# Moving the second part's mask work from VectorE to GpSimd and ScalarE

## The chip, the cores and the metric

The kernel runs on one core of one Trainium2 chip. The metric is the device time of one execution in microseconds (us), median of three runs. A core has five engines that run side by side and meet only at semaphores: TensorE (PE in the profile), VectorE (DVE), ScalarE (ACT), GpSimd (POOL) and SyncE (SP), which issues most of the DMAs.

## The reference

128 graphs of 64 nodes with 256 features go through two graph networks. The first is one attention layer with 8 heads. The second, which this case is about, has 3 layers, each with one attention head and a feed-forward part:

```
mask = adjacency.astype(float32) + eye(n) > 0          # self loops added
for l in range(3):
    scores = si[:, :, None] + sj[:, None, :] + attn_b[l]
    scores = where(scores >= 0, scores, 0.2 * scores)
    scores = where(mask, scores, -inf)
    attn   = softmax(scores, axis=-1)
    h      = layernorm(x + attn @ x, g1[l], beta1[l])
    x      = layernorm(h + gelu(h @ W1[l] + b1[l]) @ W2[l] + b2[l], g2[l], beta2[l])
```

`adj` holds int32 zeros and ones. The mask depends on the graph alone, so one mask serves all three layers.

## The kernel before

Two graphs share the 128 partitions. Four such pairs (512 nodes) are a group; there are 16 groups. The first part goes over 64 pairs in a loop and leaves its result in memory. The second part takes the groups four at a time: a lap is 4 groups times 3 layers, 12 units, and there are 4 laps, so 48 units U = 0 to 47. The unit within a lap is `s`; `layer_group(s)` gives its layer (`s // 4`) and group (`s % 4`).

Each unit has 8 chunks, c = 0 to 7. A chunk is a product with W1 into a PSUM bank (`hidden`, L773, 6 matmuls with 512 columns), a gelu in place (`gelu`, ACT L874), a rounded copy (`high`, ACT L879, tile hid_hi), its remainder (`low`, DVE L1057, tile hid_lo), and, two chunks later, a product with W2 (`output`, L797, 12 matmuls with 256 columns). After the eighth `hidden` TensorE runs `output` for chunks 5, 6 and 7 one behind the other; the last of them needs `low` of chunk 7.

Between the chunks each engine runs, in an order written out by hand, the attention of coming units. On DVE (`some` in `second_vector`): sums and statistics, `scores` of unit U + 2 (L1139 to L1147), and for U + 3 `make_mask` (only if that unit is of layer 0), `dots_of` (8 dot products a unit, L1100: one between chunks 6 and 7, in two instructions, and three pairs behind chunk 7) and `diagonal`. On POOL (`some` in `second_gpsimd`): `make_base`, `scale_y`, `finish` (last layer only), `scale_n`, `post`. On ACT, exp of U + 2 at the end of the unit.

`make_mask(i, s)` waits for the group's load (`s_in`), adds `node_of` (a float tile with 1 on the diagonal) to the int32 adjacency into `mask_sum` (L1109), and turns zeros into -1e30 and the rest into 0 (L1112), in `mask`, which stays for three layers. It runs between `low` of chunks 4 and 5 in the units 9 to 12, 21 to 24 and 33 to 36, once in the middle and once late in unit 0, and twice in the tail of the first part: 16 times. In other units it adds 2 to the semaphore `s_sc` by itself (`dve.sem_inc`).

The first part's last ten steps (`tail(tau)`, tau from NT = 64 on) are mixed with the start of the second part. TensorE's `bias` products (L812) stand there too.

## Time and profile before

| | |
|---|---|
| median of 3 runs | 1536.05 us (1535.99 to 1536.13) |
| profiled execution, its own time | 1535.7 us |
| its span, first to last instruction | 1533.5 us |
| PE busy | 1490.6 us, 97% |
| PEld busy | 1272.8 us, 83% |
| DVE busy | 1390.3 us, 91% |
| ACT busy | 1102.2 us, 72% |
| POOL busy | 898.8 us, 59% |
| granted TensorE clock, mean | 0.987 |

How to read it: busy is time with an instruction of that engine under way. The share is a mean over the whole span; what bounds a stretch is seen where an engine stops and for whom it waits. Engines run their own lists in order, so a wait holds everything that stands behind it in that list.

### The profile page before, as it was taken

Reading aid. Unit: us, or ns where it says so; the run is one execution under the profiler, and the core shown is the slowest. Engines: PE = TensorE matmul, PEld = TensorE weight load, DVE = VectorE, ACT = ScalarE, POOL = GpSimd, SP = SyncE. Lnnn points to the kernel's source line nnn. Section 1 sums busy time; section 2 is a strip of 40 time slices with the busy share of each in tenths; the row PEclk is TensorE's granted clock in tenths of the full one; section 3 lists DMA queues with packets and bytes.
Section 4 is the critical chain, followed back from the end, with each engine's and each line's share of the span. In section 5 each row is a group of like instructions: output and inputs, shape, how many; then the busy total and the mean of one; then the engine's idle time right before and its main releaser. Section 6 shows DMA issues by size and latency. Waiting matters only on the chain. (4 is left out here: it accounts for less than half of the span.)

```text
span 1533.5 us, 35213 instructions
## 1 busy us (share of the span) xinstructions
PE 1490.6 (97%) x11360; PEld 1272.8 (83%) x11360; DVE 1390.3 (91%) x4315; ACT 1102.2 (72%) x1948; POOL 898.8 (59%) x1006
## 2 busy tenths in 40 slices
PE   5899999899999999999999999999999999999997
PEld 3677777778888888888989888988888888888887
DVE  7999999879999999999898999898999998989864
ACT  5788888267777767677777676777777677777774
POOL 5799998336463647463636465645455655455565
PEclk9999999599999999999999999999999999999999
DMA  6643334500000102110001121100011211000001
GB/s 199 167 136 124 134 124 132 169 21 15 8 15 10 47 25 87 35 42 8 15 24 33 38 74 42 36 8 15 25 32 40 71 49 29 8 15 8 15 29 55
DMA packets 70890, 82.79 MB, mean 54 GB/s; under 512 B 29280, under 2 KB 54112, under 8 KB 70752
## 3 DMA queue, kind: packets, MB, share of 16 engines
q1 hardware_dynamic: 69120, 74.76, 16.9%
q0 software_dynamic: 816, 3.15, 0.7%
q10 hardware_dynamic: 816, 3.15, 0.5%
q8 instruction: 74, 1.21, 0.3%
q14 instruction: 64, 0.52, 0.1%
HBM read 38.95 MB, written 25.17 MB: 42 GB/s over the span
## 5 line engine op out<-in xcount | busy, mean ns | idle before, releaser
L874 ACT ACTIVATE bank<-bank,b_col 128x512 f32<-128x512 f32 x384 | 252.0, 656 | 282.9 <-PE bank L773 281.7
L797 PE MATMUL bank<-w_hi,hid_hi 128*128 128x256 f32 x1528 | 433.9, 284 | 6.7 <-DVE hid_lo L1057 6.7
L797 PE MATMUL bank<-w_lo,hid_hi 128*128 128x256 f32 x1528 | 431.8, 283 | 0.0
L797 PE MATMUL bank<-w_hi,hid_lo 128*128 128x256 f32 x1528 | 431.8, 283 | 0.0
L1057 DVE TENSOR_TENSOR hid_lo<-bank,hid_hi 128x512 fp32r<-128x512 f32 x384 | 262.2, 684 | 66.6 <-ACT hid_hi L879 65.3
L773 PE MATMUL bank<-nT_hi,w_hi 128*128 128x512 f32 x768 | 317.3, 413 | 1.2 <-DVE nT_lo L1186 1.2
L797 PEld LDWEIGHTS bank<-w_hi,hid_hi 128*128 128x128 f32 x1528 | 291.2, 191 | 22.9 <-DVE hid_lo L1057 9.7
L773 PE MATMUL bank<-nT_lo,w_hi 128*128 128x512 f32 x768 | 303.4, 395 | 0.0
L773 PE MATMUL bank<-nT_hi,w_lo 128*128 128x512 f32 x768 | 301.9, 393 | 0.0
L797 PEld LDWEIGHTS bank<-w_lo,hid_hi 128*128 128x128 f32 x1528 | 291.5, 191 | 11.8
L797 PEld LDWEIGHTS bank<-w_hi,hid_lo 128*128 128x128 f32 x1528 | 291.4, 191 | 0.0
L1007 POOL TENSOR_TENSOR rs_f<-ve_f,minus_half 128x4 f32<-128x4 f32 x47 | 47.8, 1017 | 412.6 <-DVE ve_f L1086 412.6
L1100 DVE CUSTOM_DVE_ANT_0 raw_weights<-xin,att_row 128x256 f32<-128x256 f32 x384 | 240.4, 626 | 10.0
L879 ACT CAST hid_hi<-bank 128x512 fp32r<-128x512 f32 x384 | 225.9, 588 | 10.7
L773 PEld LDWEIGHTS bank<-nT_hi,w_hi 128*128 128x128 f32 x768 | 145.9, 190 | 37.3 <-issue 13.4
L773 PEld LDWEIGHTS bank<-nT_hi,w_lo 128*128 128x128 f32 x768 | 145.0, 189 | 33.5
L773 PEld LDWEIGHTS bank<-nT_lo,w_hi 128*128 128x128 f32 x768 | 146.4, 191 | 16.4
L994 POOL TENSOR_TENSOR raw_weights<-raw_weights,c_row 128x512 f32<-128x512 f32 x96 | 133.4, 1409 | 0.0
L884 ACT ACTIVATE y_tok<-y_tok,nm_f,rs_f 128x256 f32<-128x256 f32 x188 | 102.9, 596 | 35.2 <-POOL nm_f L1009 35.2
L1000 POOL TENSOR_TENSOR rs_a<-ve_a,minus_half 128x4 f32<-128x4 f32 x48 | 48.7, 1014 | 133.4 <-DVE ve_a L1180 133.4
L990 POOL TENSOR_TENSOR raw_weights<-raw_weights,g_row 128x512 f32<-128x512 f32 x96 | 123.4, 1306 | 5.8 <-PE bank L763 4.2
L901 ACT ACTIVATE raw_weights<-raw_weights,nm_a,rs_a 128x256 f32<-128x256 f32 x192 | 99.8, 593 | 5.8 <-POOL nm_a L1002 5.7
(144 smaller groups left out, 3124.5 us busy)
## 6 DMA issues: line engine op xcount, KB each, us to landing
raw_weights<-xin SPq DMA_DIRECT2D x96, 128.0 KB, 2.3
xin<-in_x_dram SPq DMA_DIRECT2D x16, 512.0 KB, 4.0
first_block_out<-x_res SPq DMA_DIRECT2D x16, 512.0 KB, 2.7
second_block_in<-x_act SPq DMA_DIRECT2D x16, 512.0 KB, 3.7
xin<-second_block_in SPq DMA_DIRECT2D x16, 512.0 KB, 3.9
x_fin<-first_block_out SPq DMA_DIRECT2D x16, 512.0 KB, 4.1
out_dram<-x_fin SPq DMA_DIRECT2D x15, 512.0 KB, 2.9
xh_other<-xh SPq DMA_DIRECT2D x128, 33.0 KB, 1.9
```

Of the source, the lines that this page charges most:

```text
L773: mm = pe.matmul(HID[(CF * s + c) % 3][:], w[:, l, k, c * P:(c + 1) * P], a[:, s % 2, k, :], start=(k == 0 and p == 0), stop=(k == KD - 1 ...
L797: mm = pe.matmul(FF[t // 2][:, (t % 2) * D:(t % 2 + 1) * D], a[:, r, t * P:(t + 1) * P], w[:, l, c, :], start=(c == 0 and t % 2 == 0 and p ...
L874: act.activation(h[:], h[:], ACT.Gelu, bias=b1_col[:, l, c:c + 1]).then_inc(s_gelu, 1)
L879: act.copy(hid_hi[:, (CF * s + c) % HRING, :], HID[(CF * s + c) % 3][:]).then_inc(s_hi, 1)
L884: act.activation(y_tok[:, par, t, :], y_tok[:, par, t, :], ACT.Identity, bias=nm_f[:, t:t + 1], scale=rs_f[:, t:t + 1]).then_inc(s_yn, 1)
L901: act.activation(n_tok[:, s % 2, t, :], n_tok[:, s % 2, t, :], ACT.Identity, bias=nm_a[:, t:t + 1], scale=rs_a[:, t:t + 1]).then_inc(s_n, 1)
L990: pool.tensor_tensor(base[:, h], base[:, h], g1_row[:, l].unsqueeze(1).broadcast_to([P, TG // 2, D]), ALU.mult).then_inc(s_base, 1)
L994: pool.tensor_tensor(base[:, h], base[:, h], c1_row[:, l].unsqueeze(1).broadcast_to([P, TG // 2, D]), ALU.add).then_inc(s_base, 1)
L1000: pool.tensor_tensor(rs_a[:], ve_a[:], minus_half[:], ALU.pow).then_inc(s_rsa, 1)
L1007: pool.tensor_tensor(rs_f[:], ve_f[:], minus_half[:], ALU.pow).then_inc(s_rsf, 1)
L1057: dve.tensor_tensor(hid_lo[:, r, :], HID[(CF * s + c) % 3][:], hid_hi[:, r, :].bitcast(F32), ALU.subtract).then_inc(s_split, 1)
L1100: dve.tensor_tensor_reduce(dots, x_cur[:, g, t, :], att_row[:, l, j, :], 1.0, 0.0, ALU.mult, ALU.add, dst[:, t:t + 1]).then_inc(s_dots, 1)
```

## The change

The mask is made by two other engines. At the start DVE makes an int32 copy of the diagonal (`node_int`) and a column `far` with 1e30. POOL adds `node_int` to the loaded adjacency in place (`add_loops`), at the end of its work in the units where DVE made the mask before. ACT makes `mask` as relu(-1e30 * edges + 1e30) between `high` of chunk 1 and `gelu` of chunk 2 of the following unit (`make_mask`, for unit U + 2); it is 1e30 where there is no edge and 0 elsewhere, so `scores` subtracts it. DVE's `make_mask` is gone with the 2-step count; `scores` waits for `s_mask` in layer 0. In the diff the first `make_mask` and the first `tail` are ScalarE's, `add_loops` and the second `tail` GpSimd's, and the removed `make_mask` was VectorE's.

```diff
+        node_int = sb("node_int", [P, N], I32)
+        far = sb("far", [P, 1])
-        mask_sum = in_raw(2048, TG, N)
...
                 dve.tensor_copy(ident_r[:], ident[:]).then_inc(q_identr, 1)
+                dve.memset(far[:], -NEG).then_inc(q_loops, 1)
+                dve.tensor_copy(node_int[:], node_of[:]).then_inc(q_loops, 1)
...
+                def make_mask(i, s):
+                    l, g = layer_group(s)
+                    V = i * SLOTS + s
+                    act.wait_ge(s_edges, V // SLOTS * QG + g + 1)
+                    at_least(act, s_sc, 7 * (V - QG + 1))
+                    act.activation(mask[:, g].rearrange("p t j -> p (t j)"), adj_raw[:, g].rearrange("p t j -> p (t j)"),
+                                   ACT.Relu, bias=far[:], scale=NEG).then_inc(s_mask, 1)
...
                 def tail(tau):
+                    if tau == NT + 4:
+                        act.wait_ge(q_loops, 2)
+                        make_mask(0, 0)
...
                         keep_attn(0, 0)
+                        make_mask(0, 1)
...
                             high(U, s, c)
+                            if nxt2 and c == 1 and layer_group(s + 2)[0] == 0:
+                                make_mask(i, s + 2)
...
+                def add_loops(i, s):
+                    l, g = layer_group(s)
+                    V = i * SLOTS + s
+                    pool.wait_ge(s_in[g], 32 * (V // SLOTS + 1))
+                    pool.tensor_tensor(adj_raw[:, g], adj_raw[:, g], node_int[:].unsqueeze(1).broadcast_to([P, TG, N]),
+                                       ALU.add).then_inc(s_edges, 1)
...
                             post(i, s - 1)
+                        if nxt3 and layer_group(s + 3)[0] == 0:
+                            add_loops(i, s + 3)
+
+                def tail(tau):
+                    if tau == NT + 2:
+                        pool.wait_ge(q_loops, 2)
+                        add_loops(0, 0)
+                    if tau == NT + 5:
+                        add_loops(0, 1)
+                    if tau == NT + 8:
+                        add_loops(0, 2)
...
-                score = Steps(dve, s_sc, 9)
+                score = Steps(dve, s_sc, 7)
...
-                def make_mask(i, s):
-                    l, g = layer_group(s)
-                    V = i * SLOTS + s
-                    score.unit(V)
-                    if l == 0:
-                        dve.wait_ge(s_in[g], 32 * (i + s // SLOTS + 1))
-                        score.done(dve.tensor_tensor(mask_sum, adj_raw[:, g], node_of[:].unsqueeze(1).broadcast_to([P, TG, N]),
-                                                     ALU.add))
-                        score.wait()
-                        score.done(dve.tensor_scalar(mask[:, g], mask_sum, 0.0, NEG, ALU.is_le, ALU.mult))
-                        score.wait()
-                    else:
-                        score.k += 2
-                        dve.sem_inc(s_sc, 2)
...
-                    score.resume(V, 3)
+                    score.resume(V, 1)
                     score.wait()
+                    if l == 0:
+                        dve.wait_ge(s_mask, (V // SLOTS * QG + g + 1))
...
-                                                            mask[:, g, t, :], ALU.add, ALU.add))
+                                                            mask[:, g, t, :], ALU.add, ALU.subtract))
```

DVE's list in unit 10, before. A dot product (L1100) stands as "ISA"; L1057 is `low`, L1139 to L1147 `scores`, L1109 and L1112 the mask, L1186 the remainder of the turned rows.

```order
L1139 SCALAR_TENSOR_TENSOR raw_weights<-bank,src_b,raw_weights 128x64 x4
L1142 SCALAR_TENSOR_TENSOR raw_weights<-raw_weights 128x256
L1144 TENSOR_REDUCE top<-raw_weights 128x4
L1147 TENSOR_TENSOR raw_weights<-raw_weights,top 128x256
L1057 TENSOR_TENSOR hid_lo<-bank,hid_hi 128x512
L1109 TENSOR_TENSOR raw_weights<-adjin,node_of 128x256
L1112 TENSOR_SCALAR raw_weights<-raw_weights 128x256
L1057 TENSOR_TENSOR hid_lo<-bank,hid_hi 128x512
L1186 SCALAR_TENSOR_TENSOR nT_lo<-bank_7,g_col,nT_hi 128x512 x2
L1057 TENSOR_TENSOR hid_lo<-bank,hid_hi 128x512
L1100 ISA raw_weights,s_src<-xin,att_row 128x256
```

The same place in the changed kernel, where `low` is L1093, `scores` L1163 to L1171 and the dot products L1136:

```order
L1163 SCALAR_TENSOR_TENSOR raw_weights<-bank,src_b,raw_weights 128x64 x4
L1166 SCALAR_TENSOR_TENSOR raw_weights<-raw_weights 128x256
L1168 TENSOR_REDUCE top<-raw_weights 128x4
L1171 TENSOR_TENSOR raw_weights<-raw_weights,top 128x256
L1093 TENSOR_TENSOR hid_lo<-bank,hid_hi 128x512 x2
L1210 SCALAR_TENSOR_TENSOR nT_lo<-bank_7,g_col,nT_hi 128x512 x2
L1093 TENSOR_TENSOR hid_lo<-bank,hid_hi 128x512
L1136 ISA raw_weights,s_src<-xin,att_row 128x256
```

`low` of chunks 4 and 5 are now neighbours; nothing else on DVE changes its place.

POOL's list from `post` of unit 9 to `scale_y` of unit 10, before (L967 and L971 `post`, L990 and L994 `make_base`):

```order
L1002 TENSOR_TENSOR nm_a<-ng_a,rs_a 128x4
L967 TENSOR_TENSOR y_tok<-y_tok,g_row 128x512 x2
L971 TENSOR_TENSOR y_tok<-y_tok,beta_row 128x512 x2
L990 TENSOR_TENSOR raw_weights<-raw_weights,g_row 128x512 x2
L994 TENSOR_TENSOR raw_weights<-raw_weights,c_row 128x512 x2
L1007 TENSOR_TENSOR rs_f<-ve_f,minus_half 128x4
```

And in the changed kernel:

```order
L1027 TENSOR_TENSOR nm_a<-ng_a,rs_a 128x4
L985 TENSOR_TENSOR y_tok<-y_tok,g_row 128x512 x2
L989 TENSOR_TENSOR y_tok<-y_tok,beta_row 128x512 x2
L1019 TENSOR_TENSOR adjin<-adjin,node_int 128x256
L1008 TENSOR_TENSOR raw_weights<-raw_weights,g_row 128x512 x2
L1012 TENSOR_TENSOR raw_weights<-raw_weights,c_row 128x512 x2
L1032 TENSOR_TENSOR rs_f<-ve_f,minus_half 128x4
```

The integer add stands between `post` and the next unit's `make_base`.

ACT's list at the start of unit 10 in the changed kernel (L878 gelu, L883 hid_hi, L900 `keep_attn`, L888 `norm_y`); before, the same rows stand there without L907:

```order
L878 ACTIVATE bank<-bank,b_col 128x512
L900 COPY raw_weights<-bank 128x256
L883 CAST hid_hi<-bank 128x512
L878 ACTIVATE bank<-bank,b_col 128x512
L883 CAST hid_hi<-bank 128x512
L907 ACTIVATE raw_weights<-adjin,far 128x256
L878 ACTIVATE bank<-bank,b_col 128x512
L883 CAST hid_hi<-bank 128x512
L888 ACTIVATE y_tok<-y_tok,nm_f,rs_f 128x256 x2
```

No table load stands at the relu; both lists hold 96 table loads in all.

## Rows read from the trace of the kernel before

**Rows 1.** Busy time by stretch: from:to, length, then PE, PEld, DVE, ACT, POOL.

```profile
588.00:619.00 31.00, 30.16 (x203) 26.10 (x202) 30.24 (x92) 21.27 (x35) 15.70 (x14) 1.00 0.15 43
650.00:681.00 31.00, 31.00 (x211) 27.53 (x210) 28.87 (x88) 23.69 (x41) 18.46 (x18) 1.00 0.15 44
```

**Rows 2.** Timeline of PE, `output` where it waited: start, length, engine, line, ..., [idle before].

```profile
332.04 0.39 PE L797 MATMUL bank<-w_hi,hid_hi 128*128 128x256 f32 x1 [1.31 <-DVE hid_lo L1057]
...
562.73 0.39 PE L797 MATMUL bank<-w_hi,hid_hi 128*128 128x256 f32 x1 [0.48 <-DVE hid_lo L1057]
...
588.53 0.39 PE L797 MATMUL bank<-w_hi,hid_hi 128*128 128x256 f32 x1 [0.42 <-DVE hid_lo L1057]
...
1249.20 0.39 PE L797 MATMUL bank<-w_hi,hid_hi 128*128 128x256 f32 x1 [0.42 <-DVE hid_lo L1057]
```

**Rows 3.** Timeline of PE, `turn_n`, once a unit: units 0, 1, 9, 13.

```profile
325.50 1.03 PE L763 MATMUL bank<-ident,raw_weights 128*128 128x128 f32 x8
...
352.66 1.04 PE L763 MATMUL bank<-ident,raw_weights 128*128 128x128 f32 x8
...
554.15 1.03 PE L763 MATMUL bank<-ident,raw_weights 128*128 128x128 f32 x8
...
657.39 1.03 PE L763 MATMUL bank<-ident,raw_weights 128*128 128x128 f32 x8
```

**Rows 4.** Timeline of DVE in unit 10, from the mask on.

```profile
580.29 0.91 DVE L1109 TENSOR_TENSOR raw_weights<-adjin,node_of 128x256 f32<-128x256 int32 x1
581.23 1.27 DVE L1112 TENSOR_SCALAR raw_weights<-raw_weights 128x256 f32<-128x256 f32 x1
582.53 0.69 DVE L1057 TENSOR_TENSOR hid_lo<-bank,hid_hi 128x512 fp32r<-128x512 f32 x1
...
585.06 1.38 DVE L1100 CUSTOM_DVE_ANT_0 raw_weights<-xin,att_row 128x256 f32<-128x256 f32 x1
...
586.48 1.39 DVE L1100 CUSTOM_DVE_ANT_0 raw_weights<-xin,att_row 128x256 f32<-128x256 f32 x1
...
587.80 0.68 DVE L1057 TENSOR_TENSOR hid_lo<-bank,hid_hi 128x512 fp32r<-128x512 f32 x1
588.40 0.41 DVE L1100 CUSTOM_DVE_ANT_0 raw_weights<-xin,att_row 128x256 f32<-128x256 f32 x1
```

**Rows 5.** Timeline of DVE in unit 13, `low` of chunk 7.

```profile
663.97 0.69 DVE L1057 TENSOR_TENSOR hid_lo<-bank,hid_hi 128x512 fp32r<-128x512 f32 x1 [0.19 <-ACT hid_hi L879]
```

**Rows 6.** Groups by line, DVE: count, busy us, mean ns, idle before.

```profile
L1112 DVE TENSOR_SCALAR raw_weights<-raw_weights 128x256 f32<-128x256 f32 x16 | 17.8, 1111 | 0.5
L1109 DVE TENSOR_TENSOR raw_weights<-adjin,node_of 128x256 f32<-128x256 int32 x16 | 13.6, 849 | 0.0
```

**Rows 7.** Groups by line, POOL.

```profile
L469 POOL TENSOR_TENSOR dst_diag<-node_of,a_dst 128x256 f32<-128x256 f32 x128 | 77.2, 623 | 0.0
```

**Rows 8.** Groups by line, ACT: norm with two per-partition columns, exp with none.

```profile
L901 ACT ACTIVATE raw_weights<-raw_weights,nm_a,rs_a 128x256 f32<-128x256 f32 x192 | 99.8, 593 | 5.8 <-POOL nm_a L1002 5.7
L890 ACT ACTIVATE raw_weights<-raw_weights 128x256 f32<-128x256 f32 x48 | 20.1, 418 | 2.0 <-DVE raw_weights L1147 1.4
```

**Rows 9.** Timeline of POOL at the same place: `make_base` behind `post`.

```profile
582.31 2.60 POOL L990 TENSOR_TENSOR raw_weights<-raw_weights,g_row 128x512 f32<-128x512 f32 x2
584.87 2.71 POOL L994 TENSOR_TENSOR raw_weights<-raw_weights,c_row 128x512 f32<-128x512 f32 x2
```

**Rows 10.** Timeline of ACT, gelu of chunk 2 in a unit that follows.

```profile
595.88 0.66 ACT L874 ACTIVATE bank<-bank,b_col 128x512 f32<-128x512 f32 x1 [1.33 <-PE bank L773]
```

**Rows 11.** Timeline of DVE: first mask, in the tail, and the second of unit 0.

```profile
267.04 0.42 DVE L1109 TENSOR_TENSOR raw_weights<-adjin,node_of 128x256 f32<-128x256 int32 x1
...
328.45 1.52 DVE L1109 TENSOR_TENSOR raw_weights<-adjin,node_of 128x256 f32<-128x256 int32 x1
```

**Rows 12.** Timeline of PE in the tail, first matmul of a step.

```profile
269.06 0.47 PE L345 MATMUL bank<-no_edge,ident_r 128*128 128x512 f32 x1 [0.15 <-DVE leaky L527]
```

**Rows 13.** Timeline of DVE at the second part's start, first residual.

```profile
292.56 1.66 DVE L1165 SCALAR_TENSOR_TENSOR raw_weights<-bank,row_inv,xin 128x256 f32<-128x256 f32 x4 [1.61 <-PE bank L754]
```

More of the change, by code:

```diff
@@ L192, in graph_net @@
             q_st = sem("first_stored")
-            q_zero = sem("first_filled")
+            q_zero, q_loops = sem("first_filled"), sem("self_loops_made")
             q_mv, q_rs, q_nmr, q_h = sem("q_mean_var"), sem("q_rstd"), sem("q_shift"), sem("q_h")
@@ L616, in graph_net @@
             s_nT, s_nhi, s_nlo, s_base = sem("nT"), sem("nT_hi_ready"), sem("nT_lo_ready"), sem("base_ready")
+            s_edges, s_mask = sem("edges_with_loops"), sem("mask_made")
             s_b, s_g2, s_c1 = sem("bias_rows_loaded"), sem("g2_rows_loaded"), sem("c1_row_made")
@@ L1046, in after @@
                         pool.tensor_tensor(nm_f[:, half], ng_f[:, half], rs_f[:, half], ALU.mult).then_inc(e_nm, 1)
-                first_gpsimd(pool, lambda tau: None)
+                first_gpsimd(pool, tail)
                 slots(pool, before, some, after)
             def second_vector(dve):
-                score = Steps(dve, s_sc, 9)
+                score = Steps(dve, s_sc, 7)
                 def low(U, s, c):
@@ L1101, in dots_of, with diagonal @@
                                                      ALU.mult, ALU.add, dst[:, t:t + 1]).then_inc(s_dots, 1)
-                def make_mask(i, s):
+                def diagonal(i, s):
                     l, g = layer_group(s)
@@ L1106, in make_mask @@
                     score.unit(V)
-                    if l == 0:
-                        dve.wait_ge(s_in[g], 32 * (i + s // SLOTS + 1))
-                        score.done(dve.tensor_tensor(mask_sum, adj_raw[:, g], node_of[:].unsqueeze(1).broadcast_to([P, TG, N]),
-                                                     ALU.add))
-                        score.wait()
-                        score.done(dve.tensor_scalar(mask[:, g], mask_sum, 0.0, NEG, ALU.is_le, ALU.mult))
-                        score.wait()
-                    else:
-                        score.k += 2
-                        dve.sem_inc(s_sc, 2)
-                def diagonal(i, s):
-                    l, g = layer_group(s)
-                    V = i * SLOTS + s
                     dve.wait_ge(s_dots, 2 * TG * (V + 1))
@@ L1191, in tail @@
                         dve.tensor_copy(same_graph_r[:], same_graph[:]).then_inc(s_samer, 1)
-                    if tau == NT + 3:
+                    if tau == NT + 4:
                         dve.wait_ge(s_w2lo, NT - HEAD)
-                        make_mask(0, 0)
-                    if tau == NT + 4:
                         dve.wait_ge(s_rows, 16 * 3)
@@ L1203, in tail @@
                     if tau == NT + 7:
-                        make_mask(0, 1)
                         dots_of(0, 1, range(0, 2))
@@ L1242, in some @@
                         low(U, s, 1)
-                        if U == 0:
-                            make_mask(0, 2)
                         if nxt:
@@ L1260, in some @@
                             scores(0, 2)
-                        if nxt3:
-                            make_mask(i, s + 3)
                         low(U, s, 5)
```

## The prediction

> **What bounds the kernel now.** I read the busy time by stretch first. Through the second part TensorE is busy in every microsecond of most stretches, as in 650 to 681 us, but not where units 9 to 12 run: in 588 to 619 it is busy 30.16 of 31 us while DVE is busy 30.24 [rows 1]. Elsewhere DVE has some 2 us of air in 31; there it has less than 1. So the kernel is bound by TensorE, and in a few places by DVE.
>
> The timeline of PE then shows what the idle time waits for. In `output` it stops once in each of units 9 to 12, 21 to 24 and 33 to 36, 12 times for 0.42 us (the first 0.48), each time for hid_lo, the work of DVE; and once in unit 0, for 1.31 us [rows 2]. These are just the units in which DVE makes a mask. The first matmul behind a gap also starts the pipeline anew, so the gap is less than the whole loss. The whole loss is read from the period of the units: from unit 1 to unit 9 it is (554.15 - 352.66) / 8 = 25.19 us, from unit 9 to 13 103.24 us for four, or 25.81, and from unit 0 to 1 27.16 us [rows 3].
>
> **How the mask makes the gap.** In unit 10 the two mask instructions take DVE from 580.29 to 582.53, 2.24 us, with `low` of chunk 5 behind them. The list then runs without a rest to `low` of chunk 7 at 587.80 to 588.48 [rows 4], and TensorE, which was ready 0.42 us before 588.53, starts right after it [rows 2]. The control is unit 13: it has no mask, but the rest of a boundary unit (the last layer's extra add on POOL, the load of a new group). There `low` of chunk 7 waits for ACT, not DVE [rows 5], and TensorE has no gap [rows 1]. So the gap is the mask's, not the boundary's.
>
> **The change part by part.** DVE loses 16 times 849 ns and 16 times 1111 ns, 31.4 us of work [rows 6]. What that is worth depends on the place.
>
> Units 9 to 12 and their two repeats: 2.24 us less DVE work ahead of a `low` that was 0.42 us late. DVE stops being last, TensorE's own pace holds, and the period falls from 25.81 to 25.19: 103.24 - 4 x 25.19 = 2.5 us a lap, three laps, 7.5 us. No more than that is had, since TensorE is the next limit at once; the remaining 1.8 us a unit become idle time of DVE. Within ordinary units the period may differ by some 0.1 us with how POOL and DVE meet, so I put 0.8 us on either side of the 7.5.
>
> Unit 0: the mask late in it starts at 328.45, its add takes 1.52 us [rows 11], and the gap behind is 1.31 [rows 2]; the period is 27.16 - 25.19 = 1.97 above the ordinary [rows 3]. `low` of chunks 6 and 7 come closer to the end of ACT's work there, so I take 1.9. The other mask of unit 0 stands ahead of a wait for TensorE and is worth nothing.
>
> The tail: the first mask stands at 267.04 [rows 11], amid the last steps of the first part. TensorE's wait for DVE behind it is 0.15 us [rows 12]; the loop through TensorE and ACT is as tight. Later TensorE works through its bias products, and DVE waits 1.61 us for it at 292.56 [rows 13], so nothing that DVE gains before gets through. I take 0.15; the bounds are 0 and the whole mask, about 1.2 (267.04 to the next instruction).
>
> What is added. POOL gets 16 integer adds of 128x256. The trace has no integer add on POOL; its float product with the same shape and a broadcast operand takes 623 ns [rows 7], and one instruction of `make_base`, with 128x512, 1.3 us [rows 9]. I take 0.65 us and keep 0.3 and 1.3 as ends. It stands right behind `post`, and `make_base` starts at 582.31 without a rest and ends at 587.58 [rows 9]. What needs that is `take_y` of the next unit on DVE, which stands behind `low` of chunk 7 (587.80 to 588.48) and six more dots of 0.41 us [rows 4], so not before 590.9: over 3 us of room cover the shift of 0.65. If the cover were gone, each us would be TensorE's.
>
> The add has a price on DVE as well. A dot product takes 0.41 us when POOL rests and 1.38 when it works: the two between chunks 6 and 7 do the latter, the one behind chunk 7 the former, since POOL ends at 587.58 [rows 4, 9]. With POOL busy 0.65 us longer, one more dot pair meets it and grows by up to 1 us. That is less than the 2.24 us that DVE gives back, and it falls behind `low` of chunk 7, where TensorE has the whole of the next unit's first chunk ahead of it. The two dots before chunk 7 already wait about a whole POOL instruction each (1.38 and 1.39 against 2.71 / 2 = 1.36 [rows 9]), so a shift can hardly make them longer. Sum for this item: 0, bound 0.3 us a unit or 3.6 us.
>
> The Trainium skill (SBUF — State Buffer, Who interferes with whom) has the rule for it: the second port of DVE is shared with GpSimd as an exclusive lock, and the later one waits for the other's whole instruction. By this rule an add costs DVE at most its own length, and only if it is in flight when an instruction with two SBUF inputs comes up; the sum would stay as it is. The trace agrees as far as it goes: the dots grow by about one POOL instruction less their own start.
>
> ACT gets 16 relus of 128x256 with one per-partition column. Exp without a column takes 418 ns, the norm with two 593 [rows 8]; I take 0.5. It stands ahead of the gelu of chunk 2, where ACT waits 1.33 us for TensorE [rows 10]. So it is hidden with 0.8 us to spare; without the cover it would be 12 x 0.5 = 6 us. In unit 0 the gelu of chunk 2 has no such rest, but its `low` comes some microseconds later behind a wait of DVE for TensorE. A table load would break this, at two loads a mask, but the compiled list has none at the relu. POOL's wait for the load stands a unit or more behind the place where the load is issued, as DVE's did. The waits of ACT for POOL's add, and of DVE for the mask, each have a quarter of a unit or more.
>
> The same skill (ScalarE: Activation LUTs, Rules for kernel authors) says to put relu on VectorE, not on ScalarE, because it is faster there. By it the change would be a loss per operation. Here it is the idle engine that counts: ACT is busy 21 us of 31 where DVE is busy 30 [rows 1], and the 849 + 1111 ns on DVE [rows 6] are more than the relu's estimate anyway.
>
> At the start DVE gets a memset and a small copy, below 0.4 us together, while it waits for the first load: 0.
>
> **The sum.** 7.5 + 1.9 + 0.15 = 9.5 us. The profiled execution took 1535.7 us with a span of 1533.5 us; it becomes 1526.2 with 1524.0. The median of the runs lies 0.35 above it: 1526.5 us.
>
> **Rivals.** (a) The lock eats part of it. POOL's instructions land 0.65 us later in units 9 to 12, some dot ahead of chunk 7 waits for one more of them, and `low` of chunk 7 stays 0.3 us late. For it: a dot is three times as long under POOL [rows 4]. Against: the shift moves POOL's ends, not their number, and the dots there are at 1.4 already. Price 12 x 0.3 = 3.6: 1530.1 us.
>
> (b) More comes back than the sum has: the whole 1.2 us of the first mask [rows 11] pass through the tail instead of 0.15, and the 0.8 us of the periods fall to the good side. 1.05 + 0.8 = 1.85 us more: 1524.7 us. For it: DVE does get ahead there, and the steps of the tail hand work back and forth. Against: the 1.61 us wait for TensorE [rows 13].
>
> (c) The change doesn't do what it says: the period of units 9 to 12 belongs to the boundary (new loads, last layer's add on POOL). Then only unit 0 gains: 1534.1 us. Against it stands unit 13 [rows 5].
>
> (d) Slower: POOL's integer add is a slow path. In unit 10 it would start at 582.31 [rows 9]. The first dot behind `low` of chunk 6 waits for its end, the second for the next POOL instruction (1.3 us), and `low` of chunk 7, 0.68 us long, must start by 588.53 - 0.42 - 0.68 = 587.43 for TensorE to have no gap [rows 2, 4]. With 1.3 us for the second dot's wait and 0.5 for its own work, 582.3 + L + 1.8 = 587.4: L = 3.3 us is free. Each us above is lost 12 times. Against the 9.5 us gained (0.8 a unit) it decides from L = 4.1 us. At 5 us: 12 x 1.7 = 20 us lost, 1547 us. Nothing in the trace is near: 623 ns for this shape [rows 7].
>
> **How the numbers follow.** Forecast 0.75, its own range 1525.3 to 1528.0 (0.8 for the periods, 0.4 for unit 0 and the tail, and part of the lock). (a) 0.12, (b) 0.07, (c) 0.03, (d) 0.03. The range of 8 in 10 takes in (a) and the near half of (b): 1524.7 to 1530.5. A difference under 0.2%, 3.1 us, cannot be told from none with a measurement of this kernel. The forecast, (a) and (b) are faster by more than that: 0.93 with a little off for mixtures. Within: (c) and the off part, 0.04. Slower: (d), 0.03.
>
> **What would show it.** Right: no gap of PE for hid_lo in units 9 to 12, 21 to 24, 33 to 36 and at most 0.1 us in unit 0; four periods of 100.7 us where 103.24 stood; `low` of chunk 7 waiting for ACT in these units; POOL's add at 0.6 to 0.8 us; the relu at 0.5 us and the rest before the gelu of chunk 2 shorter by that; DVE busy 31 us less, but for dots grown behind chunk 7. Wrong: gaps left in these units (then (a), with dots ahead of chunk 7 above 1.4 us), an add above 1.3 us, a first residual that moved by more than 1 us from 292.56 to either side (then the tail's 0.15 is wrong).

## The result, and the profile after

The changed kernel takes 1525.41 us (median of 4 runs, 1523.56 to 1525.83) against 1536.02 us for the kernel before (4 runs, 1535.93 to 1536.13), a ratio of 0.9929 with the 95% interval 0.9911 to 0.9946. The forecast was 1526.5 us. The profiled execution took 1523.56 us, the shortest of the four; its span is 1521.7 us, 11.8 us less than before.

From the page of the changed kernel: the busy line, then three groups (busy us and mean ns of one behind the first bar, idle time ahead of them behind the second).

```profile
PE 1485.7 (98%) x11360; PEld 1270.5 (83%) x11360; DVE 1369.0 (90%) x4285; ACT 1108.9 (73%) x1964; POOL 911.4 (60%) x1022
...
L801 PE MATMUL bank<-w_hi,hid_hi 128*128 128x256 f32 x1528 | 432.1, 283 | 0.1
...
L1093 DVE TENSOR_TENSOR hid_lo<-bank,hid_hi 128x512 fp32r<-128x512 f32 x384 | 261.1, 683 | 77.5 <-ACT hid_hi L883 76.6
...
L1136 DVE CUSTOM_DVE_ANT_0 raw_weights<-xin,att_row 128x256 f32<-128x256 f32 x384 | 246.9, 643 | 10.0
```

TensorE no longer waits in `output` (0.1 us in all, 6.7 before), and `low` (L1093) waits 76.6 us for ACT, where it was 65.3 before. The stretch of busy time that answers to [rows 1], in the changed kernel:

```profile
588.00:619.00 31.00, 31.00 (x218) 27.00 (x218) 29.18 (x89) 22.05 (x38) 18.18 (x18) 1.00 0.15 44
```

TensorE is busy in all 31 us, and DVE, busy 29.18 us, has some air. The periods come from the same instruction as in [rows 3], `turn_n`, here for units 0, 1, 9 and 13 of the changed kernel (start, us, engine, line):

```profile
323.55 1.04 PE L767 MATMUL bank<-ident,raw_weights 128*128 128x128 f32 x8
...
349.04 1.04 PE L767 MATMUL bank<-ident,raw_weights 128*128 128x128 f32 x8
...
550.45 1.03 PE L767 MATMUL bank<-ident,raw_weights 128*128 128x128 f32 x8
...
650.95 1.04 PE L767 MATMUL bank<-ident,raw_weights 128*128 128x128 f32 x8
```

Units 9 to 12 take 100.50 us (103.24 before), unit 0 25.49 (27.16), units 1 to 8 201.41 (201.49). Over the whole span, read in this way:

| stretch | before | after | gain |
|---|---|---|---|
| four units with masks, three laps | 103.24, 103.19, 103.19 | 100.50, 100.60, 100.51 | 8.0 |
| period of unit 0 | 27.16 | 25.49 | 1.67 |
| first `turn_n` to that of unit 0 | 25.53 | 23.99 | 1.54 |
| start of the first `turn_n` | 299.97 | 299.56 | 0.41 |
| all other units | 830.42 | 830.25 | 0.2 |

The third row was not in the prediction. In it the granted clock differs. The last three numbers of each line are the granted clock, the DMA share and GB/s, first for the kernel before, then for the changed one:

```profile
307.00:310.00 3.00, 1.66 (x5) 0.94 (x4) 0.00 (x0) 2.94 (x4) 2.05 (x2) 0.82 0.45 126
310.00:313.00 3.00, 2.07 (x7) 1.74 (x8) 1.10 (x3) 2.96 (x5) 2.90 (x3) 0.75 0.02 7
313.00:316.00 3.00, 3.00 (x22) 2.61 (x25) 1.32 (x3) 1.88 (x4) 0.00 (x0) 0.68 0.00 0
...
308.10:308.60 0.50, 0.50 (x3) 0.13 (x1) 0.00 (x0) 0.47 (x2) 0.50 (x1) 1.00 0.38 143
```

```profile
307.00:310.00 3.00, 1.64 (x4) 0.72 (x3) 0.00 (x0) 2.94 (x4) 3.00 (x3) 0.72 0.53 143
310.00:313.00 3.00, 2.48 (x15) 2.23 (x16) 1.10 (x3) 2.96 (x6) 1.66 (x2) 1.00 0.00 0
313.00:316.00 3.00, 3.00 (x28) 2.12 (x27) 1.83 (x4) 1.77 (x4) 0.00 (x0) 1.00 0.01 3
...
308.10:308.60 0.50, 0.50 (x2) 0.00 (x0) 0.00 (x0) 0.47 (x2) 0.50 (x1) 0.50 0.58 135
```

The engine comes out of a stretch at half its full clock (1.2 of 2.4 GHz, 0.50). Before, it rises and falls back once more before it stays up; after, it rises and stays. The last line of each group shows another difference: TensorE works until 308.6 us in both and then waits about 2 us for ACT, but before, the clock is up while it still works, and after, it comes up only when the work has ended.

The added work, all 16 of each (shortest, median and longest in ns), and where they run in unit 9 and the start of unit 10 of the changed kernel:

```profile
L1019 POOL TENSOR_TENSOR adjin<-adjin,node_int x16: 716/733/922, 265.9 to 1232.2; 128x256 int32<-128x256 int32 x16
L907 ACT ACTIVATE raw_weights<-adjin,far x16: 494/512/531, 272.4 to 1243.4; 128x256 f32<-128x256 int32 x16
```

```profile
552.55 0.74 POOL L1019 TENSOR_TENSOR adjin<-adjin,node_int 128x256 int32<-128x256 int32 x1
553.25 2.54 POOL L1008 TENSOR_TENSOR raw_weights<-raw_weights,g_row 128x512 f32<-128x512 f32 x2
```

```profile
554.22 0.69 DVE L1093 TENSOR_TENSOR hid_lo<-bank,hid_hi 128x512 fp32r<-128x512 f32 x1 [1.00 <-ACT hid_hi L883]
554.83 1.25 DVE L1136 CUSTOM_DVE_ANT_0 raw_weights<-xin,att_row 128x256 f32<-128x256 f32 x1
...
556.11 1.40 DVE L1136 CUSTOM_DVE_ANT_0 raw_weights<-xin,att_row 128x256 f32<-128x256 f32 x1
...
557.44 0.68 DVE L1093 TENSOR_TENSOR hid_lo<-bank,hid_hi 128x512 fp32r<-128x512 f32 x1
558.04 0.91 DVE L1136 CUSTOM_DVE_ANT_0 raw_weights<-xin,att_row 128x256 f32<-128x256 f32 x1
...
582.16 0.69 DVE L1093 TENSOR_TENSOR hid_lo<-bank,hid_hi 128x512 fp32r<-128x512 f32 x1 [0.35 <-ACT hid_hi L883]
```

```profile
564.22 0.51 ACT L907 ACTIVATE raw_weights<-adjin,far 128x256 f32<-128x256 int32 x1
565.65 0.66 ACT L878 ACTIVATE bank<-bank,b_col 128x512 f32<-128x512 f32 x1 [0.92 <-PE bank L777]
```

In unit 9 `low` of chunk 6 (554.22) waits 1.00 us for ACT, where before it had no rest. `low` of chunk 7 (557.44) still starts right behind a dot, 6.99 us after the unit's `turn_n`; before it was 7.85. So of the 2.24 us taken off DVE only 0.86 reach it, and most of the rest is that wait ahead of it. In units 10 to 12 it waits for ACT, 0.35 us in unit 10 (582.16), 0.25 and 0.16 in the next two; over the three laps it does so in 7 of the 12 units. The dot behind it is 0.91 us in unit 9 instead of 0.41, as POOL works longer.

### The profile page after: what moved, and what is told of

Its sections match the earlier page's. It is cut to its first block, busy times and chain, and to the rows that moved or that the text cites. A ratio compares the mean times of both kernels' runs of the same rounds, so it can differ in the third digit from the quotient of the medians.

```text
span 1521.7 us, 35183 instructions
## 1 busy us (share of the span) xinstructions
PE 1485.7 (98%) x11360; PEld 1270.5 (83%) x11360; DVE 1369.0 (90%) x4285; ACT 1108.9 (73%) x1964; POOL 911.4 (60%) x1022
## 4 chain that ended last, share of the span: by engine, by line
PE 94%; DVE 2%; DMA 1%; issue 1%; ACT 1%; SPq 0%; POOL 0%; ACTq 0%; DVEq 0%; POOLq 0%
PE bank L801 36%; PE bank L777 35%; PE bank L758 3%; PE bank L361 3%; PE bank L351 3%; PE bank L767 3%; PE bank L319 2%; PE bank L336 2%; PE bank L349 2%; DMA adjin<-in_adj_dram 1%; PE bank L329 1%; PE bank L346 1%; PE bank L816 1%; PE bank L746 1%; PE bank L738 0%
## 5 line engine op out<-in xcount | busy, mean ns | idle before, releaser
L878 ACT ACTIVATE bank<-bank,b_col 128x512 f32<-128x512 f32 x384 | 251.9, 656 | 258.0 <-PE bank L777 257.0
L1093 DVE TENSOR_TENSOR hid_lo<-bank,hid_hi 128x512 fp32r<-128x512 f32 x384 | 261.1, 683 | 77.5 <-ACT hid_hi L883 76.6
L1136 DVE CUSTOM_DVE_ANT_0 raw_weights<-xin,att_row 128x256 f32<-128x256 f32 x384 | 246.9, 643 | 10.0
L883 ACT CAST hid_hi<-bank 128x512 fp32r<-128x512 f32 x384 | 226.2, 589 | 10.6
L888 ACT ACTIVATE y_tok<-y_tok,nm_f,rs_f 128x256 f32<-128x256 f32 x188 | 102.9, 596 | 44.0 <-POOL nm_f L1034 44.0
```

Source lines behind the costliest of these rows:

```text
L878: act.activation(h[:], h[:], ACT.Gelu, bias=b1_col[:, l, c:c + 1]).then_inc(s_gelu, 1)
L883: act.copy(hid_hi[:, (CF * s + c) % HRING, :], HID[(CF * s + c) % 3][:]).then_inc(s_hi, 1)
L888: act.activation(y_tok[:, par, t, :], y_tok[:, par, t, :], ACT.Identity, bias=nm_f[:, t:t + 1], scale=rs_f[:, t:t + 1]).then_inc(s_yn, 1)
L1093: dve.tensor_tensor(hid_lo[:, r, :], HID[(CF * s + c) % 3][:], hid_hi[:, r, :].bitcast(F32), ALU.subtract).then_inc(s_split, 1)
L1136: dve.tensor_tensor_reduce(dots, x_cur[:, g, t, :], att_row[:, l, j, :], 1.0, 0.0, ALU.mult, ALU.add, dst[:, t:t + 1]).then_inc(s_dots, 1)
```

## Experiments

Periods are those of `turn_n` in each kernel's trace; in two traces of the changed kernel they agree to about 0.1 us, while totals of one kernel spread by 2 to 4 us. "Four units" are 9 to 12, 21 to 24 and 33 to 36, in this order. The kernel before, timed beside them, took 1534.23 us (1532.72 to 1536.42) beside the repeat, the 12 late masks, the first four and the adds in all other units; 1534.76 (1534.54 to 1536.75) beside the tail's two, unit 0's two, the kernel without the added work and the one with an add on DVE; 1534.74 (1534.48 to 1536.99) beside the other four. A ratio is against the one beside it.

### The change again

No edit.

> The changed kernel once more, for its spread and a second trace. Theory A (DVE was last in 13 units, TensorE is now): no gap of PE for hid_lo again, four periods of 100.5 us in units 9 to 12, whatever the total. Theory B (part of the gain is TensorE's clock at the second part's start, which comes back at one of several moments): runs spread over 2 us, and the trace shows the clock back at full speed between 308 and 317 us; a run with an early return is at 1523.6, one with a late return at 1525.8.

Measured 1525.56 us (1523.63 to 1525.95), ratio 0.9938 (0.9925 to 0.9952). Four units 100.52, 100.72, 100.50; unit 0 25.46; stretch ahead of it 23.99. The gain repeats, at 8.7 us by the medians where the first comparison had 10.6. The periods say 9.7 (8.0 for the late masks and 1.67 for unit 0); what the totals add or lack is their spread.

### Which masks give what

Four kernels move only some masks. `moved(V)` chooses; the others are made by VectorE at the old places:

```diff
+            def moved(V):
+                return V >= QG        # the 12 late ones; the others have V < QG, V in (0, 1), V in (2, 3)
...
+                    if l == 0 and not moved(V):
+                        score.done(dve.tensor_tensor(mask_sum, adj_raw[:, g], node_of[:].unsqueeze(1).broadcast_to([P, TG, N]), ALU.add))
+                        score.wait()
+                        score.done(dve.tensor_scalar(mask[:, g], mask_sum, 0.0, -NEG, ALU.is_le, ALU.mult))
```

The 12 late masks alone:

> Only the 12 masks of laps 1 to 3 are moved; the first four stay on VectorE as before. Theory A: 12 gaps gone, the one of unit 0 stays: 1536.0 - 8.0 = 1528.0 us (1527.7 to 1528.4). Theory B: nothing changes before 554 us, so the clock does there what it did before, and the runs spread by 0.3 us at most. Rival (the gain belongs to the start): 1534 us or more.

The first four alone:

> Only the first four masks are moved (two in the first part's tail, two in unit 0); the 12 later ones stay on VectorE. Theory A: the gap of unit 0 goes (1.7 us) and 0.4 us of the tail: 1533.9 us; 12 gaps of 0.42 us stay. Theory B: the spread of over 1 us of the changed kernel is here too, between 1532.3 and 1534.5 us, with the moment of the clock's return. Rival (no clock effect): 1533.9 within 0.2 us.

The two of the tail:

> Only the first two masks, those made in the tail of the first part, are moved to GpSimd and ScalarE; the masks of unit 0 and of units 9 to 12 stay on VectorE. The stretch from the first turn_n of the second part to that of unit 0 took 25.5 us before and 24.0 us after the change, with TensorE's granted clock back at 1.00 from 316 us on before and from 310 us on after; in the run with the first four moved it was 24.0 too, in the run with the 12 late ones moved 25.5. Theory A (the clock's return hangs on how the steps of the tail follow each other, so on the first two masks): about 24.0 us here, the gap of 1.3 us of unit 0 stays, the period of unit 0 is 27.2; total about 2.0 us less than before. Rival B (it hangs on unit 0's masks): 25.5 us, total about 0.2 to 0.4 us less than before. Units 9 to 12 at 103.2 us for four under both.

The two of unit 0:

> Only the two masks made in unit 0 are moved to GpSimd and ScalarE; the two of the tail and those of units 9 to 12 stay on VectorE. Theory A (clock's return hangs on the tail's masks): the stretch ahead of unit 0 takes 25.5 us as before, the period of unit 0 falls from 27.16 to about 25.5 us with no gap of 1.3 us in output; total about 1.7 us less than before. Rival B (unit 0's masks): the stretch takes 24.0 us, total about 3.2 us less. Units 9 to 12 at 103.2 us for four under both.

| moved | us (runs) | ratio, interval | ahead of unit 0 | unit 0 | four units |
|---|---|---|---|---|---|
| 12 late | 1527.74 (1525.42 to 1527.87) | 0.9951 (0.9937 to 0.9965) | 25.50 | 27.16 | 100.66, 100.51, 100.51 |
| first four | 1532.79 (1531.64 to 1533.48) | 0.9988 (0.9979 to 0.9997) | 24.01 | 25.47 | 103.20, 103.20, 103.20 |
| two of the tail | 1535.20 (1533.46 to 1535.39) | 0.9999 (0.9989 to 1.0008) | 24.02 | 27.15 | 103.22, 103.18, 103.11 |
| two of unit 0 | 1533.60 (1532.10 to 1534.79) | 0.9987 (0.9978 to 0.9997) | 25.47 | 25.46 | 103.21, 103.20, 103.14 |

By the periods the 12 late masks are 8 us and the two masks of unit 0 are 1.7 us, separately and in sum. Two forecasts of totals failed: with the 12 late masks alone the runs were to spread by 0.3 us at most and spread by 2.5, and with the tail's masks alone 2.0 us were to be gained and the total didn't move. With the tail's masks alone moved, the gap of unit 0 stays (PE of that kernel, idle before in brackets):

```profile
330.32 0.39 PE L808 MATMUL bank<-w_hi,hid_hi 128*128 128x256 f32 x1 [1.29 <-DVE hid_lo L1104]
```

The stretch ahead of unit 0 came out in these four as the theory of the tail's masks has it, 24.0 or 25.5. But seven kernels below are the whole change up to that point, and four of them show 25.5. So that theory falls as a rule: over 14 traces the stretch takes 23.98 to 24.02 us in 7 and 25.47 to 25.53 in 7. In all of the first kind the granted clock is 1.00 from 313 to 316 us, in all of the second 0.53 to 0.80. All three traces without the tail's masks moved are of the second kind, of the eleven with them four. Whether the change shifts the odds, 14 traces don't tell. What does divide all 14 is where the clock's rise falls against TensorE's pause: in the seven of 25.5 us it comes 0.2 to 0.6 us before TensorE stops (before: up from 308.1, stop at 308.66), in the seven of 24.0 us up to 0.7 us after it has stopped. Why it then falls again no run tests. This and where the first `turn_n` begins (298.64 to 300.52) is what spreads between executions.

### The added work taken out

In the 12 late units neither `add_loops` nor `make_mask` runs; these units take over masks made earlier:

```diff
+                    if V >= QG:
+                        return
```

> As the changed kernel, but from the second lap on no mask is made: neither GpSimd's add nor ScalarE's relu of the 12 later masks is there, and those graphs take the masks of the first lap (that part of the computation is left out). The prediction costs the added work at nothing: periods of units 9 to 12 as with the change, 100.5 to 100.7 us for four, and the total within 0.3 us of the changed kernel. Rival (the added work costs something through the dots it lengthens or through ACT's order): periods shorter by 0.1 us a unit or more, 1.2 us or more in total. The dot behind low of chunk 7 should be back at 0.41 us, and ACT's wait ahead of the gelu of chunk 2 at 1.3 us.

Measured 1525.06 us (1524.91 to 1525.21), ratio 0.9936 (0.9918 to 0.9954); four units 100.69, 100.63, 100.72. No shorter than with the work (100.50, 100.60, 100.51). The 384 dots together take 237.0 us here, 246.9 with the change and 240.4 before: the adds lengthen DVE's dots by 9.9 us, 0.8 a unit, and TensorE doesn't notice. Costing them at nothing was right.

### GpSimd's add in all other units too

```diff
+                        elif U > 0 and not (last and s == SLOTS - 1):
+                            filler()     # one int32 add of 128x256, result unused
```

> The changed kernel with an integer add of the same size on GpSimd in all other units too, at the same place; its result is not used. In the changed kernel units 9 to 12 run at 25.12 us each, and the others alternate between 25.12 and 25.24. Theory C: the slow ones are those in which the two dots ahead of chunk 7 wait for two whole GpSimd instructions (2.9 us), and an add in front shifts GpSimd's instructions so that they wait less: all units at 25.12, 1.0 to 1.7 us less than the changed kernel. Rival (the alternation has nothing to do with GpSimd's phase, or more GpSimd work costs DVE more): the same time or up to 4 us more.

Measured 1524.56 us (1522.90 to 1525.50), ratio 0.9936 (0.9923 to 0.9950). The ordinary units take 201.01, 201.12 and 201.35 (201.41, 201.35, 201.33 with the change). The dots go to 261.5 us. So an add costs nothing there either. Theory C, all units at 25.12 (201.0 for eight), holds in the first of the three stretches only; that the add would help is not shown, as 0.6 us in all is within what such units vary.

### How much of DVE's time is spare

At the old place of the mask, in the 12 late units, DVE makes an add (first kernel) or the add and the tensor_scalar that made the mask (second), for no use:

```diff
+                    dve.tensor_tensor(mask_sum, loops, node_of[:].unsqueeze(1).broadcast_to([P, TG, N]), ALU.add).then_inc(s_fa, 1)
+                    dve.wait_ge(s_fa, k)
+                    # second kernel only:
+                    dve.tensor_scalar(spare, mask_sum, 0.0, NEG, ALU.is_le, ALU.mult).then_inc(s_fb, 1)
```

> The changed kernel, and on VectorE, at the place where the mask was made, one float add of 128x256 in the 12 late units (0.85 us with its wait about 0.95), whose result nobody reads. The prediction's sum says that of the 2.24 us taken off VectorE 0.42 us and a restart made TensorE's loss (0.6 us a unit) and the rest, some 1.6 us, became idle time of VectorE. Theory A (slack): 0.95 us more fits in, no gap of PE, four periods at 100.5 to 100.8 us, the total as with the change. Rival B (VectorE's work there is proportional to what TensorE loses, by the exclusive meeting with GpSimd): some 0.6 x 0.95 / 2.24 = 0.25 us a unit, 3 us in total.

> The changed kernel, and on VectorE, at the place where the mask was made, both operations that made it (float add of 128x256, then tensor_scalar of the same size, 2.2 us together) in the 12 late units, their result read by nobody. GpSimd's add and ScalarE's relu are there too. Theory A (the gain of these units is VectorE's time at that place alone): 12 gaps of PE of about 0.42 us are back, four periods at 103.2 us, total 8.0 us above the changed kernel. Rival B (part of the gain came from another order of the waits or of the buffers): less than 6 us come back. Above 8.5 us: GpSimd's added instruction meets VectorE there and costs more, which the prediction put at nothing.

Add alone: 1526.34 us (1525.77 to 1526.88), ratio 0.9943 (0.9925 to 0.9961), four units 101.19, 100.84, 101.20: 1.6 us over the change in all, 0.13 a unit. That is between the theories: less than rival B's 3 us, but the 0.95 us is not free. The list of PE's waits shows none for hid_lo in these units, but five of them (11, 12, 24, 35, 36) are 0.3 us longer, 1.4 of the 1.6 us, and there the delay is at `output` of chunk 2 in the unit that follows. DVE and PE of this kernel, then PE of the changed one at the same place:

```profile
622.89 0.67 DVE L1095 TENSOR_TENSOR hid_lo<-bank,hid_hi 128x512 fp32r<-128x512 f32 x1
```

```profile
623.62 0.39 PE L803 MATMUL bank<-w_hi,hid_hi 128*128 128x256 f32 x1
```

```profile
621.58 0.28 PE L801 MATMUL bank<-w_hi,hid_hi 128*128 128x256 f32 x1
```

`low` ends at 623.56, and `output` starts 0.06 us behind it, 21.08 us after the `turn_n` of unit 11, with a first matmul of 0.39 us instead of 0.28. With the change it starts 20.87 to 20.88 us after `turn_n`, and `low` of chunk 2 ends 0.07 to 0.9 us ahead of that. So in these units DVE's reserve is smallest there, not at chunk 7: its work runs without a wait from chunk 7 to chunk 2 of the next unit, and what is added before chunk 7 and isn't taken up in its waits for ACT arrives there.

Both: 1531.04 us (1528.95 to 1531.22), ratio 0.9974 (0.9963 to 0.9985), four units 102.47, 102.48, 102.48: 5.8 of the 8.0 us are back. By the number that is rival B (less than 6), but the gaps of theory A are there too, and what is missing comes, as the trace below shows, from where POOL's boundaries fall and not from order or buffers. The gaps are 9, not 12; the first of each lap, in unit 9, is missing. In that kernel's trace of unit 9, first DVE, then POOL:

```profile
554.91 0.68 DVE L1095 TENSOR_TENSOR hid_lo<-bank,hid_hi 128x512 fp32r<-128x512 f32 x1
555.51 0.83 DVE L1138 CUSTOM_DVE_ANT_0 raw_weights<-xin,att_row 128x256 f32<-128x256 f32 x1
...
556.39 1.40 DVE L1138 CUSTOM_DVE_ANT_0 raw_weights<-xin,att_row 128x256 f32<-128x256 f32 x1
...
557.72 0.68 DVE L1095 TENSOR_TENSOR hid_lo<-bank,hid_hi 128x512 fp32r<-128x512 f32 x1
```

```profile
552.77 0.78 POOL L1021 TENSOR_TENSOR adjin<-adjin,node_int 128x256 int32<-128x256 int32 x1
553.50 2.56 POOL L1010 TENSOR_TENSOR raw_weights<-raw_weights,g_row 128x512 f32<-128x512 f32 x2
556.03 2.91 POOL L1014 TENSOR_TENSOR raw_weights<-raw_weights,c_row 128x512 f32<-128x512 f32 x2
```

The first dot comes up at 555.51 and ends 0.3 us after POOL's next boundary (556.03): 0.83 us. In the kernel before it was so, DVE first:

```profile
559.23 1.40 DVE L1100 CUSTOM_DVE_ANT_0 raw_weights<-xin,att_row 128x256 f32<-128x256 f32 x1
...
562.00 0.68 DVE L1057 TENSOR_TENSOR hid_lo<-bank,hid_hi 128x512 fp32r<-128x512 f32 x1
```

```profile
556.49 2.60 POOL L990 TENSOR_TENSOR raw_weights<-raw_weights,g_row 128x512 f32<-128x512 f32 x2
559.06 2.73 POOL L994 TENSOR_TENSOR raw_weights<-raw_weights,c_row 128x512 f32<-128x512 f32 x2
```

There the dot came up just behind a boundary (559.06) and took 1.40. The shift by POOL's add is worth 0.57 us to `low` of chunk 7, whose start is 7.26 us after `turn_n` instead of 7.85, and unit 9 takes 25.27 us instead of 25.86. The other three take 25.70 to 25.76 instead of 25.80. So what the mask's time on DVE costs hangs on how it falls against POOL's boundaries: the same work at the same place cost 8.0 us without POOL's add (and ACT's relu) and 5.8 with them.

### How long GpSimd's add could have been

In the 12 late units the add is made 4 and 7 times:

```diff
+                    times = 4 if V >= QG else 1      # 7 in the second kernel
+                    for n in range(times):
...
+                        add = pool.tensor_tensor(adj_raw[:, g], adj_raw[:, g], node_int[:].unsqueeze(1).broadcast_to([P, TG, N]), ALU.add).then_inc(s_adds, 1)
```

> GpSimd's integer add made four times in the 12 late units, one after the other (4 x 0.72 us, 2.9 us with their handover instead of 0.72; the values are then wrong in three of them and the mask with it, its time is not). The prediction had 3.3 us free at this place. Theory A: the total stays within 0.5 us of the changed kernel, no gap of PE, only VectorE's dots ahead of chunk 7 wait longer. Rival B (each added instruction lengthens a dot): 0.3 to 1 us a unit, 4 to 12 us in total.

> GpSimd's integer add made seven times in the 12 late units, 5.1 us with the handover (the values and so the mask are then wrong). By the prediction's formula for a slow add 3.3 us are free and each us above is lost 12 times: (5.1 - 3.3) x 12 = 22 us above the changed kernel, with gaps of PE of about 1.8 us in output for hid_lo. Rival B: seven short instructions let VectorE's dots in between, one each, where one long one would not; then low of chunk 7 waits for two short ones (0.7 us each) alone, and what is late is make_base and take_y of the next unit, with over 3 us to spare (5.1 - 0.7 = 4.4 us of shift against 3.3 + 0.7): 0 to 5 us in total.

Four: 1547.98 us (1547.86 to 1548.22), ratio 1.0087 (1.0070 to 1.0104), four units 108.34, 108.45, 108.10, 2.1 us more for each unit once the lap has settled (27.23). Seven: 1571.46 us (1570.57 to 1572.17), ratio 1.0241 (1.0224 to 1.0258), four units 115.36, 115.57, 116.00. By the periods the 12 units take 23.3 and 45.3 us more than with the change. The theories had 0.5 or 4 to 12 for four adds, and 22 or 0 to 5 for seven: all failed, and the place at which they looked too. In unit 9 with four adds, first DVE, then POOL, then the gap on PE:

```profile
557.95 0.69 DVE L1102 TENSOR_TENSOR hid_lo<-bank,hid_hi 128x512 fp32r<-128x512 f32 x1 [0.91 <-ACT hid_hi L883]
558.56 1.26 DVE L1145 CUSTOM_DVE_ANT_0 raw_weights<-xin,att_row 128x256 f32<-128x256 f32 x1
...
559.87 1.39 DVE L1145 CUSTOM_DVE_ANT_0 raw_weights<-xin,att_row 128x256 f32<-128x256 f32 x1
...
561.30 1.39 DVE L1145 CUSTOM_DVE_ANT_0 raw_weights<-xin,att_row 128x256 f32<-128x256 f32 x1
...
562.73 0.42 DVE L1145 CUSTOM_DVE_ANT_0 raw_weights<-xin,att_row 128x256 f32<-128x256 f32 x1
...
565.09 1.41 DVE L1116 TENSOR_TENSOR y_tok<-bank,raw_weights 128x256 f32<-128x256 f32 x4
...
566.74 0.68 DVE L1102 TENSOR_TENSOR hid_lo<-bank,hid_hi 128x512 fp32r<-128x512 f32 x1
```

```profile
553.47 3.28 POOL L1026 TENSOR_TENSOR adjin<-adjin,node_int 128x256 int32<-128x256 int32 x4
556.99 2.55 POOL L1008 TENSOR_TENSOR raw_weights<-raw_weights,g_row 128x512 f32<-128x512 f32 x2 [0.24 <-POOL adjin L1026]
559.50 2.90 POOL L1012 TENSOR_TENSOR raw_weights<-raw_weights,c_row 128x512 f32<-128x512 f32 x2
```

```profile
567.48 0.39 PE L801 MATMUL bank<-w_hi,hid_hi 128*128 128x256 f32 x1 [0.95 <-DVE hid_lo L1102]
```

`low` of chunk 7 is early: it waits 0.91 us for ACT, and with seven adds too. Late is `low` of chunk 0 of the next unit (566.74), behind the six dots, `diagonal` and `take_y`. POOL's `make_base`, moved back by 2.8 us, now meets three of those dots, and each takes 1.3 to 1.4 us instead of 0.42. `take_y` (565.09) doesn't wait for `make_base` at all, which ended at 562.40. With one add this `low` starts at 563.94, 13.49 us after `turn_n`; here at 15.37. It is 1.88 us later and TensorE has lost 0.95, so in unit 9 the change has left 0.9 us to spare there (chunk 2 can have less, above). The mask itself comes out the same, as more adds only raise the diagonal and the relu turns any edge into 0.

### ScalarE's relu four times

```diff
+                    for n in range(4 if V >= QG else 1):
...
+                        act.activation(mask[:, g].rearrange("p t j -> p (t j)"), adj_raw[:, g].rearrange("p t j -> p (t j)"), ACT.Relu, bias=far[:], scale=NEG).then_inc(s_relus, 1)
```

> ScalarE's relu made four times in the 12 late units (4 x 0.51 us, 2.05 us; each writes the same mask). The prediction hid one relu under a wait of 1.33 us ahead of the gelu of chunk 2. Theory A (that wait is all the cover): 2.05 - 1.33 = 0.7 us a unit come through, 8 us in total above the changed kernel. Rival B (VectorE reaches low of chunk 2 later than ScalarE delivers its part, so the lateness is taken up there): no gap of PE, total within 0.5 us.

Measured 1526.07 us (1524.65 to 1526.39), ratio 0.9941 (0.9924 to 0.9957); four units 100.51, 100.81, 100.51: rival B. ACT and then DVE of this kernel, start of unit 10:

```profile
566.64 2.15 ACT L913 ACTIVATE raw_weights<-adjin,far 128x256 f32<-128x256 int32 x4
568.91 0.66 ACT L878 ACTIVATE bank<-bank,b_col 128x512 f32<-128x512 f32 x1
569.60 0.59 ACT L883 CAST hid_hi<-bank 128x512 fp32r<-128x512 f32 x1
```

```profile
572.55 0.67 DVE L1101 TENSOR_TENSOR hid_lo<-bank,hid_hi 128x512 fp32r<-128x512 f32 x1
```

The wait ahead of the gelu of chunk 2 is used up, and the gelu is 0.83 us later against `turn_n` than with one relu (16.03 for 15.20). But DVE takes that chunk at 572.55, behind `residual` and its statistics, 19.67 us after `turn_n` in both kernels. A second cover lies behind the first: hid_hi is ready at 570.19 and taken 2.4 us later.

## Why the prediction was right

**Late masks, 7.5 us: 8.0.** The mechanism is as said: no gap for hid_lo is left in the 12 units, the 12 masks alone give the gain, and the same work put back brings the gaps back in 9 of 12 units. Put back beside POOL's add, that work costs 5.8 us, so 2.2 of the 8.0 hang on how DVE's dots met POOL in the kernel before; the prediction had them in its measured period without naming them. The size was 0.5 low since I took 25.19, the mean of units 1 to 8, as TensorE's own pace; mask units now take 25.12 or 25.13 nearly always. `low` of chunk 7 waits for ACT, as said, in 7 of the 12 units; in the others it starts behind a dot or with a wait under 0.15 us, with no gap of PE.

**"The remaining 1.8 us a unit become idle time of DVE": wrong as a reserve.** One add of 0.95 us already costs 0.13 us a unit. A part of the 2.24 us had turned into waits for ACT that come ahead of the dots, and the prediction looked for DVE's next deadline at chunk 7 alone, where `low` of chunk 2 of the next unit, ending 0.07 to 0.9 us ahead of `output`, can be nearer. The total did not rest on it. DVE's busy time fell by 21.3 us (1390.3 to 1369.0), not by 31: 6.5 us are longer dots and 2.8 a longer step of `scores` (L1166), the rest isn't traced.

**Unit 0, 1.9 us: 1.67**, by the two masks of unit 0 alone 1.70. The period there falls to 25.46 to 25.49, not to the 25.19 that the 1.97 was worked out from. The prediction's reading that TensorE stopped once in unit 0 missed a second wait for hid_lo, 0.23 us at 333.95; both are gone.

**The tail, 0.15 us: nothing that can be told.** The first `turn_n` starts 0.41 us earlier, but over the traces it lies anywhere from 298.64 to 300.52. The 1.54 us in the stretch behind it came through the granted clock. The prediction had no such term, and that the profiled execution had it may well be luck (7 of 14 traces had it); it is the largest part of what puts the span, 1521.7 us, 2.3 us under the 1524.0 forecast for it (1.54, 0.5 of the masks, 0.26 of the tail's start and 0.17 of other units, less 0.23 of unit 0, are 2.2).

**What is added, 0: right, with one reason wrong.** POOL's add is 0.73 us (0.65 taken), the relu 0.51 (0.5). One dot behind chunk 7 grew, as said, and without the added work the periods are the same. The exclusive lock that the Trainium skill describes (SBUF — State Buffer, Who interferes with whom) is what the dots of all these traces show: in each of them all dots above 0.46 us, 108 to 168 a trace, end 0.28 to 0.29 us behind the end of a POOL instruction. Rival (d)'s condition, a slow add, didn't come, but its price was wrong too: "3.3 us is free" looked at `low` of chunk 7 and at `make_base` for `take_y`. What POOL moves first is DVE's dots behind chunk 7, and through them `low` of the next chunk 0. POOL held for 3.5 us instead of 0.7 costs 2.1 us a unit, where that formula has 0.2. The prediction saw the dot grow, and priced one pair, not a row that ends in the next unit. With POOL held for 3.5 us the change would be a loss of 13 us against the kernel before (1547.98 to 1534.74), where (d) put the point from which it decides at 4.1.

**ACT's "0.8 us to spare": too small.** Four relus, 2.15 us, cost nothing. The rule that relu belongs on VectorE (the Trainium skill, ScalarE: Activation LUTs, Rules for kernel authors) would have left that operation on DVE. What that costs is shown by proxy only: one add back on DVE cost 1.6 us, both operations 5.8. No run here timed a relu on DVE, so the rule's claim on speed wasn't tested.

**Rivals.** (a) no gaps left: fell. (c) fell with the late masks. (b)'s time, 1524.7, lies near, but its tail gave nothing that can be told from spread; a clock outcome that I had not thought of stands in its place.

## What to carry to other kernels

Read what an engine's removed work is worth from the period of the stretch where it is last, not from its busy time: 31.4 us off DVE were 10 us of the total, and 12 of 16 masks gave four fifths of that. When you add work to an engine that shares a resource with the critical one, ask which of the critical engine's instructions the shift will now overlap, and follow each until the next hand-over to the bound engine. A wait that you hide under has its own consumer further on; look there too before you call its length the whole cover.

## What the hardware showed

- The same dot of 128x256 on DVE takes 0.42 us with POOL idle and up to 1.59 with POOL busy (the longest of 14 traces), and a dot that grew ends 0.28 us after the end of a POOL instruction (556.06 and 556.34). Adding 28 us of POOL work lifted the sum of all dots from 246.9 to 261.5 us without moving the total.
- The integer add of 128x256 on POOL takes 0.73 us, against 0.62 for the float product of that shape [rows 7].
- TensorE's granted clock came back from 0.50 in two ways with the same code up to that point, once for good or once with a fall in between, and the second costs 1.5 us. It fell again in all seven traces in which it had risen while TensorE still worked ahead of a pause of about 2 us, and in none of the seven in which it rose during the pause.
- A product behind a wait takes longer itself: 0.39 us instead of 0.28 for the first matmul of `output`, so a delay of TensorE can be 0.3 us where the wait alone, 0.2, isn't listed.
